# The softmax row totals of an attention kernel: from a GpSimd reduction with diagonal reads to one-column matmuls on TensorE

## What is computed

```python
xf = group_norm(x, gamma, beta).reshape(B, N, C)        # B 16, N 1024, C 512
q = xf @ wq + bq; k = xf @ wk + bk; v = xf @ wv + bv
scores = jnp.einsum('bnc,bmc->bnm', q, k) * C ** (-0.5)
attn = jax.nn.softmax(scores, axis=-1)
out = jnp.einsum('bnm,bmc->bnc', attn, v)
out = out @ wp + bp
return out.reshape(B, H, W, C) + residual
```

## Time and profile before

| | us |
|---|---|
| median of 3 runs | 2138.52 (2137.93 to 3012.9) |
| the profiled execution | 2139.97 |
| its span, first to last instruction | 2138.3 |
| PE busy | 2099.0 |
| DVE busy | 1798.7 |
| POOL busy | 877.3 |
| ACT busy | 743.7 |

### The profile page before, as it was taken

The page is one execution under the profiler, slowest core; times in us unless marked ns, Lnnn a source line. Parts: engine busy times, 40 slices in busy tenths (PEclk is TensorE's granted clock), DMA queues, the critical chain, the costliest instruction groups (busy, mean ns, idle before and its releaser), DMA issues.

```text
span 2138.3 us, 28427 instructions
## 1 busy us (share of the span) xinstructions
PE 2099.0 (98%) x9253; PEld 1730.9 (81%) x9253; DVE 1798.7 (84%) x2554; ACT 743.7 (35%) x1216; POOL 877.3 (41%) x475
## 2 busy tenths in 40 slices
PE   7999999999999999999999999999999999999999
PEld 5877888888888888888888788888878888888887
DVE  6898897988979888888888979889788898888865
ACT  4242332423333243332523324233332433335232
POOL 2452442524335244443524425243352434435253
PEclk9999999999999999999999999999999999999999
DMA  8003012030300203012030120303012030120101
GB/s 211 20 11 109 1 54 64 15 103 0 94 24 34 83 0 118 0 49 69 10 108 0 56 62 15 103 0 93 25 34 83 0 118 0 49 69 10 69 1 60
DMA packets 110268, 108.13 MB, mean 51 GB/s; under 512 B 8476, under 2 KB 74016, under 8 KB 110240
## 3 DMA queue, kind: packets, MB, share of 16 engines
q1 hardware_dynamic: 107984, 103.58, 16.0%
q10 hardware_dynamic: 2256, 4.20, 0.8%
HBM read 74.19 MB, written 33.55 MB: 50 GB/s over the span
## 4 chain that ended last, share of the span: by engine, by line
PE 51%; DVE 19%; issue 18%; POOL 7%; ACT 3%; DMA 0%; POOLq 0%; DVEq 0%; ACTq 0%
PE psum L1226 6%; PE psum L1228 6%; PE psum L1227 6%; PE psum L1251 5%; PE psum L1253 5%; PE psum L1252 5%; PE psum L1140 4%; PE psum L1139 4%; PE psum L1137 4%; DVE pt_lo L694 4%; POOL total_part L449 4%; DVE score L869 3%; DVE xn_lo L694 3%; POOL total_part L458 2%; PE psum L1057 2%
## 5 line engine op out<-in xcount | busy, mean ns | idle before, releaser
L1251 PE MATMUL psum<-v_hi,pt_hi 128*128 128x512 f32 x1024 | 401.4, 392 | 20.6 <-DVE pt_lo L694 17.4
L426 POOL TENSOR_TENSOR x_res<-x_res,out_bias 128x512 f32<-128x512 f32 x128 | 201.8, 1600 | 499.1 <-PE psum L1140 371.4
L1252 PE MATMUL psum<-v_lo,pt_hi 128*128 128x512 f32 x1024 | 399.2, 390 | 0.0
L1253 PE MATMUL psum<-v_hi,pt_lo 128*128 128x512 f32 x1024 | 399.0, 390 | 0.0
L694 DVE TENSOR_TENSOR pt_lo<-score,pt_hi 128x512 fp32r<-128x512 f32 x256 | 295.2, 1178 | 28.3 <-POOL total_part L449 25.0
L449 POOL TENSOR_TENSOR total_part<-total_part,score 128x512 f32<-128x512 f32 x192 | 309.1, 1610 | 16.6
L592 ACT ACTIVATE score<-psum 128x512 f32<-128x512 f32 x256 | 152.5, 596 | 342.3 <-PE psum L1228 341.9
L1251 PEld LDWEIGHTS psum<-v_hi,pt_hi 128*128 128x128 f32 x1024 | 192.6, 188 | 68.5 <-DVE pt_lo L694 25.1
L1253 PEld LDWEIGHTS psum<-v_hi,pt_lo 128*128 128x128 f32 x1024 | 192.6, 188 | 40.3
L1252 PEld LDWEIGHTS psum<-v_lo,pt_hi 128*128 128x128 f32 x1024 | 192.7, 188 | 39.1
L1226 PE MATMUL psum<-v_hi,xn_hi 128*128 128x512 f32 x512 | 201.7, 394 | 0.0
(11 more groups left out here) (162 smaller groups left out, 3992.2 us busy)
## 6 DMA issues: line engine op xcount, KB each, us to landing
x_res<-in_x_dram SPq DMA_DIRECT2D x128, 256.0 KB, 3.0
out_dram<-x_res SPq DMA_DIRECT2D x128, 256.0 KB, 2.2
x_blk<-in_x_dram SPq DMA_DIRECT2D x240, 128.0 KB, 3.2
score<-in_x_dram SPq DMA_DIRECT2D x16, 128.0 KB, 8.0
w_q<-in_L_conv_wq_dram SPq DMA_DIRECT2D x1, 1024.0 KB, 5.5
w_k<-in_L_conv_wk_dram SPq DMA_DIRECT2D x1, 1024.0 KB, 7.9
w_v<-in_L_conv_wv_dram ACTq DMA_DIRECT2D x1, 1024.0 KB, 9.1
w_p<-in_L_conv_wp_dram ACTq DMA_DIRECT2D x1, 1024.0 KB, 13.0
```

Source lines behind the costliest of these rows:

```text
L426: last = nc.gpsimd.tensor_tensor(at, at, out_bias[:, first:end], ALU.add)
L1251: nc.tensor.matmul(dst, hi[:, m, queries], v_hi[:, m, :], start=m == 0, stop=False)
L1252: nc.tensor.matmul(dst, hi[:, m, queries], v_lo[:, m, :], start=False, stop=False)
L1253: end = nc.tensor.matmul(dst, lo[:, m, queries], v_hi[:, m, :], start=False, stop=m == NT - 1)
```

## The change

The way of the last half is now that of all 32 halves. A new `total_sums` on PE sums `total_part` over the partitions by four one-column matmuls, for half 0 between v tile 7 and output tile 0, and for half 1 between output tiles 5 and 6. The totals of half 0 go to four unused columns of the bank of the group statistics (`stat`, bank 7, which is also the bank of output tiles 3 and 7), those of half 1 to bank 0 (which v tile 0 of the next image uses first). DVE's `totals` is one reciprocal that reads PSUM. POOL's `total_sum` and DVE's four diagonal reads are gone. PE has three new waits: v tile 0 of an image waits for the reciprocals of the image before, output tile 3 waits for those of half 0, and the sums of half 0 wait until the last output tile of the image before was read.

```diff
--- before.py
+++ after.py
@@ -161,7 +161,6 @@
         rstd = sb("rstd", [P, KC])
         scale_c = sb("scale_c", [P, KC])
         shift_c = sb("shift_c", [P, KC])
-        total = sb("total", [P, NT])
         total_inv = sb("total_inv", [P, NT])
 
         psum = ctx.enter_context(nc.psum_tensor("psum", [P, 8, BANK], FP32))
@@ -169,7 +168,8 @@
         o_ps = [psum[:, 4 + i, :] for i in range(TH)]
         stat = psum[:, 7, :]
         vec_ps = stat[:, KC:4 * KC]
-        last_total = psum[:, 0, 0:TH]
+
+        half_total = (stat[:, KC:KC + TH], psum[:, 0, 0:TH])
 
         s_wload = [sem(f"w_loaded{i}") for i in range(4)]
         s_small = sem("small_loaded")
@@ -230,7 +230,6 @@
         s_ptl = sem("pt_lo_ready")
         s_sum = sem("total_part_step")
         s_tt = sem("total_ready")
-        s_tot = sem("total_in_its_partition")
         s_ti = sem("total_inv_ready")
         s_o = sem("o_done")
         s_y = sem("out_tile_ready")
@@ -249,9 +248,6 @@
 
         BANK_1, BANK_6, BANK_7, BANK_5 = work[2], work[3], work[0], work[1]
 
-
-        def final_half(n, h):
-            return h == NH - 1 and isinstance(n, int) and n == B - 1
 
         def starts(n, h=0):
 
@@ -449,14 +445,6 @@
                     nc.gpsimd.tensor_tensor(total_part[:], score[h][:, 0, :] if m == 1 else total_part[:],
                                             score[h][:, m, :], ALU.add).then_inc(s_sum, 1)
 
-            def await_total_part(n, h):
-                pool.wait_ge(s_sum, (n * NH + h + 1) * (NT - 1))
-                pool.sem_inc(s_turn, 1)
-
-            def total_sum():
-
-                nc.gpsimd.partition_all_reduce(total_part[:], total_part[:], P, ADD).then_inc(s_tt, 1)
-
             def row_sum(n):
                 pool.wait_ge(s_rv, (n + 1) * KC)
                 pool.sem_inc(s_turn, 1)
@@ -516,8 +504,6 @@
                 totals(b, 0)
                 if more:
                     root(b + 1)
-                await_total_part(b, 0)
-                total_sum()
                 await_top_part(b, 1)
                 top(b, 1)
                 if starts(b):
@@ -525,10 +511,6 @@
                         residual(b, i)
                 totals(b, 1)
                 residual(b, TH)
-                if more:
-                    await_total_part(b, 1)
-                    total_sum()
-
                 for i in range(TH + 1, NT):
                     residual(b, i)
 
@@ -880,17 +862,7 @@
 
                 tiles = slice(h * TH, (h + 1) * TH)
                 dve.wait_ge(s_tt, n * NH + h + 1)
-                if final_half(n, h):
-                    nc.vector.reciprocal(total_inv[:, tiles], last_total).then_inc(s_ti, 1)
-                    return
-                for i in range(TH):
-                    sums = total_part[:, i * P:(i + 1) * P]
-                    last = nc.vector.tensor_tensor_reduce(
-                        out=sums, in0=sums, in1=ident[:], scale=1.0, scalar=0.0, op0=ALU.mult, op1=ALU.add,
-                        accum_out=total[:, h * TH + i:h * TH + i + 1])
-                last.then_inc(s_tot, 1)
-                dve.wait_ge(s_tot, n * NH + h + 1)
-                nc.vector.reciprocal(total_inv[:, tiles], total[:, tiles]).then_inc(s_ti, 1)
+                nc.vector.reciprocal(total_inv[:, tiles], half_total[h]).then_inc(s_ti, 1)
 
             def tile_out(n, i):
                 dve.wait_ge(s_ti, n * NH + i // TH + 1)
@@ -1109,6 +1081,9 @@
+                if what == ("v", 0, 0) and not starts(n):
+
+                    pe.wait_ge(s_ti, n * NH)
                 return bank_of(*what)
 
             def group_sum(n, step, rhs):
@@ -1236,6 +1211,9 @@
                 if i >= TH or not starts(n):
 
                     pe.wait_ge(s_y, n * NT + i - TH + 1)
+                if i == TH - 1:
+
+                    pe.wait_ge(s_ti, n * NH + 1)
                 if i == TH - 1 and more:
 
                     pe.wait_ge(s_pw_in, n + 2)
@@ -1252,13 +1230,16 @@
                     nc.tensor.matmul(dst, hi[:, m, queries], v_lo[:, m, :], start=False, stop=False)
                     end = nc.tensor.matmul(dst, lo[:, m, queries], v_hi[:, m, :], start=False, stop=m == NT - 1)
                 end.then_inc(s_o, 1)
-                if final_half(n, h) and i == TH + 1:
-
-                    pe.wait_ge(s_sum, (n + 1) * NH * (NT - 1))
-                    for c in range(TH):
-                        summed = nc.tensor.matmul(last_total[:, c:c + 1], total_part[:, chunk(c)], ones[:, 0:1],
-                                                  start=True, stop=True)
-                    summed.then_inc(s_tt, 1)
+                if i == TH + 1:
+                    total_sums(n, 1)
+
+            def total_sums(n, h):
+
+                pe.wait_ge(s_sum, (n * NH + h + 1) * (NT - 1))
+                for c in range(TH):
+                    summed = nc.tensor.matmul(half_total[h][:, c:c + 1], total_part[:, chunk(c)], ones[:, 0:1],
+                                              start=True, stop=True)
+                summed.then_inc(s_tt, 1)
 
             pe.wait_ge(s_const, 6)
             weight_transpose(SET_WQ, w_q, s_wload[0])
@@ -1295,6 +1276,10 @@
                         group_sum(b + 1, 1, dev[:])
                 for m in range(2, NT):
                     v_tile(b, m)
+                if not starts(b):
+
+                    pe.wait_ge(s_y, b * NT)
+                total_sums(b, 0)
                 for i in range(NT):
                     out_tile(b, i, more)
```

## The result

The change costs 6.6 us: the median is 2145.27 us (8 runs, 2143.49 to 2147.77) against 2138.64 for the kernel before on the same chip (8 runs). One of these eight took 3012.9 us; the other seven lie between 2137.48 and 2139.69. The ratio is 1.0031, with a 95% interval of 1.002 to 1.0043. The forecast was 2145, a hair slower; that held. The profiled execution took 2143.69, its span 2142.0.

What follows compares the result with a forecast made beforehand. PE, busy 98% of the span, was taken to bound the kernel. 27.3 us for 30 groups, less 19.8 for recurring waits and 0.8 for image 0, gives +6.7: median 2138.52 becomes 2145.2 us, range 2137 to 2155.

Steps and rivals of the forecast that it cites:

- The price of the groups: On PE, each added group of four one-column sums costs 0.91 us; 30 groups not hidden cost 27.3 us.
- The saving in the loop: PE's recurring waits for low parts at output tile 4 all go, saving 19.8 us, about 1.4 per loop image.
- Where DVE gets its lead: Half 0's reciprocals begin 1.21 us after v tile 7's last wide matmul, making DVE 1.0 us earlier.
- the prediction's bounds: For low parts in a loop image: no DVE gain leaves a 0.54 us cost; 1.0 or more saves all 1.45.
- The slack: Low part 6 of half 1 is ready at 1077.0, PE wants it at 1077.6: 0.6 us to spare.
- Image 0: Half 0's group hides in a 3.1 us v-tile wait, half 1's costs 0.91; low-part waits give back 0.8 us.
- Rival 1: On PE, a group of sums costs 0.65 us, not 0.91: total 2137.4 us; chance 0.15 (2135 to 2141).
- Rival 2: Low-part waits stay in part, 0.54 us in each loop image: total 2152.8 us; chance 0.15 (2149 to 2157).
- Rival 3: New PE wait at the next image's v tile 0, residuals holding DVE up by 3.3 us; 2160 to 2183; chance 0.1.
- Half 1's savings, costed at nothing: POOL's dropped reduction (3.69 us) and switches and DVE's dropped reads for half 1 save PE nothing; nobody on the path waited.

Runs made afterwards that it cites:

- the last experiment: The kernel before the change, all reductions and diagonal reads kept, with the next image's variance and norm made earlier on DVE: 2117.6 us, ratio 0.9896.

## Why the prediction was right

**The total: right, its last digit by luck.** 2145.2 was forecast and 2145.27 measured, but the interval of the ratio reaches from 4.3 to 9.2 us. By parts, the 14 images of the loop came out at +5.9 us, where 5.7 was forecast; image 0 was missed by 1.1 us, as told below.

**The price of the groups: right, slightly low.** An image of the loop without any wait and with no added group takes 128.372 us (the last experiment), and with two groups 130.244: 0.94 us for one, where 0.91 was forecast from the earlier trace rows. The difference is that the small disturbance behind a group reaches farther than the two strides of the window: from 1051.10 to 1054.32 are 3.22 us where ten strides are 2.27, so 0.95. The 28 groups of the loop cost 26.2 us against 25.5. The one of image 15 is in line with it.

**The saving in the loop: right.** 129.826 - 128.372 = 1.45 us were lost in an image by waits, and all of it came back; 1.41 was forecast. One detail of the text was wrong, though not the sum: the 15 waits of the earlier trace rows lie in the 14 images of the loop (one has two), none in image 15. An image of the loop was forecast at 130.2 us, and takes 130.24.

**Where DVE gets its lead: right, but not the whole reason.** The reciprocals begin 1.22 us after the last wide matmul, forecast 1.21, and DVE is 1.02 earlier, forecast 1.0. But the step that says "`top(b, 1)` on POOL takes the place of the removed reduction at 1047.74 instead of 1050.90, so it doesn't hold the shift back" was treated as a side condition, and the run with the unneeded reduction shows that it is one to be kept: with the same early reciprocals, `top` behind a reduction holds the shift back by 0.7 us, 0.4 of it through that run's own extra wait. What it cost was 0.29 us in an image, so at most a fifth of the 1.45. And the lead wasn't needed whole: with the diagonal reads done once DVE has hardly any left, and 0.24 us are lost, where the prediction's bounds had 0.54 for no lead at all. The rest of the wait was filled by PE's own group.

**The slack: larger than forecast.** 0.6 us to spare were forecast, 1.26 are seen in the image shown and 0.9 on average, but 0.3 in the image with least. POOL's first addition of half 1 begins 8.32 us after the last wide matmul (1059.42 - 1051.10) where it was 9.88 before (1060.50 - 1050.62): 1.56 earlier, not 1.0. The forecast took 7.5 us from the reciprocals' end to that addition; it is now 6.9 (1052.50 to 1059.42). That is not a shorter switch: over the images of the loop it took 7.1 to 7.9 us before (7.4 on average) and 6.9 to 7.9 after (7.2), and this spread is most of what makes the slack differ from image to image. Where it comes from was not tried.

**Image 0: the step failed, its sum did not.** The forecast called the group of half 0 there free, hidden by the wait of 3.1 us for a v tile, and gave back 0.8 us of the low parts' waits. In fact that wait is nearly gone (0.3 us), so the group isn't hidden, and the low parts' waits are 2.9 us instead of 1.7. The wait had been made by the removed reduction: in image 0 it lay beside DVE's `norm` and the low parts of `ab_sum`. The timeline of DVE there, before and then after:

```profile
131.43 4.91 DVE L751 TENSOR_SCALAR x_t<-x_t,scale_c,shift_c 128x1024 f32<-128x1024 f32 x4
136.26 3.33 DVE L694 TENSOR_TENSOR ab_lo<-ab_sum,ab_hi 128x512 fp32r<-128x512 f32 x4
```

```profile
129.07 3.71 DVE L733 TENSOR_SCALAR x_t<-x_t,scale_c,shift_c 128x1024 f32<-128x1024 f32 x4
132.70 2.48 DVE L676 TENSOR_TENSOR ab_lo<-ab_sum,ab_hi 128x512 fp32r<-128x512 f32 x4
```

Together 8.2 us became 6.2. The wait of 3.1 us had also cost more than itself, since the granted clock behind it was 0.51 for 3.5 us. All in all image 0 is 0.96 us shorter, where the forecast made it 0.1 longer (a group of half 1 less 0.8). The run with the unneeded reduction brings the 4.91 and the 3.33 us back, and the wait to 2.3 us, so this cause is shown.

**Rivals.** Rival 1 (0.65 us for a group) is out by the doubled groups (0.89). Rival 2 (waits that stay in part) doesn't occur in the loop of the change, but the one set of diagonal reads shows how near it was: some 0.6 us of lateness are free, and not more. Rival 3 (a new wait at v tile 0 of the next image) was farther off than forecast: DVE has the reciprocals of half 1 at 1091.02, PE begins v tile 0 at 1096.76, 5.7 us later (4.8 to 5.8 over the loop). The residuals do spread out as that rival said, and `block_sums` takes 5.83 us beside one of them instead of 4.75, which is 1.1 us where 3.3 were allowed for.

**Half 1's savings, costed at nothing: right.** 15 groups for which nobody had waited cost 15 us, the difference between the changed kernel and half 0 alone.

## What to carry to other kernels

Work that is moved to the engine that sets the time must remove a wait of that engine, group by group: here half 0's sums do, half 1's don't, and taken alone they gain 10 us and lose 17. Before such work is bought with the busiest engine's time, follow the late chain back to what holds its first link: here it was a tiny operation in a queue on another engine, and moving it, with the norm behind it, gained 23 us without adding or removing any work. In a loop, compare the distance of one step from image to image, not spans, for setup alone can differ by 2 us; and read a slack in all images, for one image showed four times that of another.

## What the runs showed of the hardware

- Four fp32 matmuls of one column, eight pairs of weight load and matmul, take 0.94 us of a stream of 512-column matmuls, and 0.89 when they stand right behind another such group: about 0.11 us for a pair, half of the 0.23 of a matmul of 512 columns.
- PARTITION_ALL_REDUCE on POOL slows DVE's TENSOR_SCALAR from SBUF to SBUF: four tiles of 128x1024 take 2.99 us alone, 4.49 beside the end of one reduction and the whole of the next, and 6.12 when they lie beside both almost from the first's start. The reductions are slower too (3.73 instead of 3.25, and 2.73 instead of 1.80). The Trainium skill, page "SBUF — State Buffer", section "Who interferes with whom", tells of a port pair that DVE and GpSimd share under an exclusive lock; these numbers agree in that each slows the other, but don't show the lock itself.
- A wait of PE can cost more than its length and the 0.27 us of its restart: behind the 3.1 us in image 0 the granted clock was 0.51 of full speed for 3.5 us, its lower level of 1.2 GHz. In the kernel with half 1 alone it was 0.51 for 5.9 us behind three waits for low parts in image 0, 2.4 us in all. In the changed kernel three such waits, 2.9 us in all, were not followed by it (1.00 from 137 to 176 us), and neither were the recurring waits of 1 to 1.4 us in the loop. What decides between the two is not shown.
